# The inverse norms of queries and keys, computed one behind the other on VectorE, in a kernel of linear attention and six local attention layers

## What is computed

```
def attn_layer(x, Wqkv, qs, ksc, Wo):
    q, k, v = split(x @ Wqkv)                 # 16 heads of 64 each
    q = q / max(norm(q), 1e-12) * qs          # per token and head
    k = k / max(norm(k), 1e-12) * ksc
    q = q * cos * scale + rotate_half(q) * sin * scale
    k = k * cos / scale + rotate_half(k) * sin / scale
    out = local_attention(q, k, v)            # windows of 32, own and the one before
    return out @ Wo
```

## Time and profile before

| | |
|---|---|
| time, median of 3 runs | 2012.22 us (2008.62 to 2013.55) |
| the profiled execution | 2012.52 us, its span 2010.7 us |
| mean granted clock of TensorE, share of full speed | 0.969 |
| busy: TensorE, VectorE, ScalarE, GpSimd | 90%, 77%, 58%, 72% |
| instructions in the trace | 85596 |

### The profile page before, as it was taken

One profiled execution on the slowest core, in us unless ns is written; L12 is line 12 of the kernel. 1 busy time (PEld: TensorE's weight loads), 2 busy tenths in 40 slices (PEclk: granted clock), 3 DMA queues, 4 the chain that ended last, 5 costly groups with the idle time before them and its releaser, 6 DMA issues. The chain is left out here.

```text
span 2010.7 us, 85596 instructions
## 1 busy us (share of the span) xinstructions
PE 1805.9 (90%) x34280; PEld 1311.9 (65%) x34280; DVE 1557.0 (77%) x2776; ACT 1164.3 (58%) x1966; POOL 1455.2 (72%) x967
## 2 busy tenths in 40 slices
PE   7774689999999999999999999999999999999995
PEld 3453466676776666766666666667676667676764
DVE  4764688887888878888788788887887888878864
ACT  2311356666666666666666666666666666666662
POOL 3221688877887778777877787778777877787771
PEclk9875899999999999999999999999999999999997
DMA  4000122223222223222223322233222232222220
GB/s 151 2 3 1 44 65 65 59 54 86 73 70 53 55 63 91 59 70 63 61 53 84 77 68 55 52 82 81 63 58 59 63 86 63 70 63 55 55 58 22
DMA packets 93581, 123.43 MB, mean 61 GB/s; under 512 B 27760, under 2 KB 41808, under 8 KB 93392
## 3 DMA queue, kind: packets, MB, share of 16 engines
q1 hardware_dynamic: 93232, 122.42, 24.2%
q10 hardware_dynamic: 288, 0.13, 0.0%
HBM read 20.74 MB, written 1.05 MB: 11 GB/s over the span
## 5 line engine op out<-in xcount | busy, mean ns | idle before, releaser
L999 POOL TENSOR_TENSOR across<-unit,turns 128x1024 f32<-128x1024 f32 x192 | 497.4, 2591 | 279.7 <-issue 268.4
L1006 POOL TENSOR_TENSOR rotated<-along,across 128x1024 f32<-128x1024 f32 x192 | 496.7, 2587 | 14.2
L1151 DVE TENSOR_REDUCE sums<-squares 128x16 f32<-128x1024 f32 x192 | 234.2, 1220 | 173.2 <-ACT squares L1054 173.1
L1247 PE MATMUL turn<-identity,rotated 128*128 128x128 f32 x1536 | 205.2, 277 | 36.4 <-POOL rotated L1006 36.4
L1247 PEld LDWEIGHTS turn<-identity,rotated 128*128 128x128 f32 x1536 | 172.6, 141 | 98.9 <-issue 83.4
L1032 POOL TENSOR_TENSOR along<-unit,turns 128x1024 f32<-128x1024 f32 x96 | 228.3, 2378 | 0.0
L1352 PE MATMUL proj_a<-w_qkv,shift_a 128*128 128x512 f32 x384 | 189.9, 617 | 36.4 <-DVE unit L1176 30.1
L1113 ACT COPY val<-proj_a 128x1024 f32<-128x1024 f32 x96 | 97.2, 1013 | 181.3 <-PE proj_a L1352 181.3
L1377 PEld LDWEIGHTS att<-o_t,w_o 128*128 128x128 f32 x1536 | 188.0, 193 | 6.1 <-issue 1.0
L1377 PE MATMUL att<-o_t,w_o 128*128 128x128 f32 x1536 | 188.3, 276 | 0.0
L1280 PE MATMUL proj_a<-w_qkv,shift_a 128*128 128x512 f32 x384 | 183.5, 601 | 4.3 <-POOL shift_a L988 3.0
(11 more groups left out here) (203 smaller groups left out, 3445.2 us busy)
## 6 DMA issues: line engine op xcount, KB each, us to landing
v_win<-val SPq DMA_DIRECT2D x1536, 64.0 KB, 2.0
w_qkv<-wqkv_dram SPq DMA_DIRECT2D x18, 512.0 KB, 3.8
w_o<-wo_dram SPq DMA_DIRECT2D x6, 512.0 KB, 4.6
where<-positions_dram SPq DMA_DIRECT2D x1, 2048.0 KB, 11.4
w_ffn<-ffn_dram SPq DMA_DIRECT2D x12, 170.5 KB, 2.3
w_ffn<-ffn_dram SPq DMA_DIRECT2D x6, 192.0 KB, 2.3
x_tok<-x_dram SPq DMA_DIRECT2D x4, 256.0 KB, 4.3
out_dram<-final SPq DMA_DIRECT2D x4, 256.0 KB, 2.4
```

Of the source, the lines that this page charges most:

```text
L999: pool.tensor_tensor(a[:, :, ::-1, :], u, table, ALU.mult).then_inc(acrossed[j], 1)
L1006: pool.tensor_tensor(rotated[j][:, :, :], along[j][:, :, :], across[j][:, :, :], ALU.add).then_inc(rotated_in[j], 1)
L1151: dve.tensor_reduce(sums[:, j, :], squares[j][:, :, :], AX.X, ALU.add).then_inc(summed[j], 1)
L1247: mm = pe.transpose(bank[:, TILE * (i % 4):TILE * (i % 4) + TILE], buffer[:, TILE * i:TILE * i + TILE], identity[:, :])
```

## The change

VectorE's part is reordered. The inverse root is computed twice, on 16 heads each, with the nine operations for the queries right behind the queries' sum of squares, and the nine for the keys behind the keys' sum. The order of VectorE in a step becomes: sum (queries), root (queries), `divide_out` twice, `unite` (queries), sum (keys), root (keys), `unite` (keys), and then as before. The semaphore `rooted` becomes one for each. All other engines' lists are unchanged.

```
-        rooted = sem("rooted")
+        rooted = [sem("q_rooted"), sem("k_rooted")]
...
                     def sum_squares(j):
                         dve.wait_ge(squared[j], p + 1)
-                        after(dve, rooted, ROOT_OPS * p)
+                        after(dve, rooted[j], ROOT_OPS * p)
...
+                    def root(j):
+                        dve.wait_ge(summed[j], p + 1)
+                        after(dve, united[j], p)
+                        inverse_root(dve, range(ROOT_OPS), sums[:, j, :], sums_min[:, j, :], inv_norm[:, j, :],
+                                     [w[:, j, :] for w in root_work], magic[:, j, :], rooted[j], ROOT_OPS * p)
+
                     def unite(j):
-                        dve.wait_ge(rooted, ROOT_OPS * p + ROOT_OPS)
+                        dve.wait_ge(rooted[j], ROOT_OPS * p + ROOT_OPS)
...
                     if live["p"]:
                         sum_squares(0)
-                        sum_squares(1)
+                        root(0)
                     if live["b"]:
                         divide_out(0)
                         divide_out(1)
                     if live["p"]:
-                        dve.wait_ge(summed[0], p + 1)
-                        dve.wait_ge(summed[1], p + 1)
-                        after(dve, united[1], p)
-                        inverse_root(dve, range(ROOT_OPS), sums[:, :, :], sums_min[:, :, :], inv_norm[:, :, :],
-                                     [w[:, :, :] for w in root_work], magic[:, :, :], rooted, ROOT_OPS * p)
                         unite(0)
+                        sum_squares(1)
+                        root(1)
                         unite(1)
```

## The result

| | before | changed |
|---|---|---|
| time, median | 2012.9 us (4 runs, 2008.6 to 2014.4) | 2782.5 us (4 runs, 2781.8 to 2783.8) |
| ratio to before | 1 | 1.383, 95% interval 1.381 to 1.385 |
| span of the profiled execution | 2010.7 us | 2780.1 us |
| mean granted clock | 0.969 | 0.861 |

The change makes the kernel slower by 770 us, 8.0 us in each of the 96 steps; 2744 us was forecast. First the changed kernel's page, busy time by engine (it answers to the earlier trace rows), and the groups by line that changed most (they answer to the earlier trace rows). In the changed file lines behind the edit are shifted: L1250 is the former L1247, L1355 the values' projection, L1362 the narrowing, L1374 the spread of the rstd, L1237 the keys' `along`.

A forecast was written before the change was run, and what follows sets the result against it. TensorE, busy 90% of the span, was taken to set the path, with the keys' `unit` deciding. 2012.5 us plus 590 for the late `unit` plus 141 for the clock gave 2744 us; range 2575 to 2900.

The forecast's parts named there:

- The likeliest case: VectorE's keys' root is blocked once by each GpSimd queries' product, then runs free; 83% chance, 2744 us.
- three products: GpSimd's `across`, `along` and `rotated` of the queries, run without a break, 7.10 us in the step before the change.
- the walk: The forecast's step-by-step timing of VectorE, GpSimd and TensorE through one changed step, ending with TensorE going on at S + 15.56.
- S: The moment in a step when VectorE starts the queries' sum of squares; other times, in us, are counted from it.
- one-meeting rival: After one blocked operation VectorE runs the keys' whole root through while GpSimd waits; 2176 us, 6% chance.
- no-meeting rival: The keys' root on VectorE is not blocked by GpSimd at all; 0.4 us a step, 2051 us, 6% chance.
- The term for the late `unit`: TensorE, behind the values' projection, waits for the keys' `unit`: 6.15 us a step with copies, 590 us over 96 steps.
- 0.15 for copies: Average us a step for queries' root operations on VectorE stretched beside GpSimd's short copies.
- The term for the clock: After idling 5.8 us TensorE works at a lower clock: 1.47 us a step, 141 us; bounds 0 and 2.5 us a step.
- What was called hidden: Later centred scores (VectorE) and ScalarE work taken at 0, at most 32 us; `along` gain and GpSimd idle off the path.
- The opposite rival: Faster: TensorE's waits for the queries' `unit` and `rotated` go, 66 us, giving 1946 us; 3% chance.
- The point of decision: S + 9.56, TensorE's instruction behind the values' projection: if the keys are united before it, nothing is lost there.

The follow-up runs named there:

- e3: Changed kernel with the keys' root rewritten as ten operations, each reading at most one tensor from SBUF, the other from PSUM: 2142.6 us, 1.066 of the kernel before.
- e4b: Changed kernel with 12 matmuls that nobody reads on TensorE behind the values' projection, filling its idle gap: 2566.7 us, 1.278 of the kernel before.
- e1: Changed kernel with GpSimd holding back the queries' `across` until the keys' root is done: 2276.2 us, 1.132 of the kernel before.
- e2: Kernel before with two separate roots, both ahead of both `unite`: 2304.5 us, 1.146 of the kernel before.

## Why the prediction was right

**The meeting.** The likeliest case said that a root operation meets each of the three products once, and that the root is free behind them. So it is, and in all 96 steps: L90 and L94 take 1.24 and 1.19 us in the mean of 192, with the queries' instances near 0.2 us, which leaves 2.2 to 2.3 us for the mean of the keys', and their maxima are 2.28 and 2.20; L96 and L98 never take over 0.18 us. The times of the walk hold too: queries united at S + 5.55 (5.63 forecast), `across` at S + 5.68 (5.76), `rotated` over at S + 12.80 (12.98). It also left open whether L92 or L94 meets the third product; it is L94, so five operations are left behind the products instead of six. The one-meeting rival (2176 us) and the no-meeting rival (2051 us) both fall with L90 and L94 at 2.2 us; e3, whose root meets nothing, came out at 2143, above the latter, as it has an operation more, waits for a bank, and waits 42 us for `hidden` behind the keys' `along`.

**The term for the late `unit`.** TensorE goes on at S + 15.28 in the odd step and S + 15.42 in the even one (1549.11 - 1533.69), where S + 15.56 and 0.15 for copies were forecast. Put at 590 us, measured 556 by e4b, 0.36 us a step too large. The keys are united at S + 15.13 in both steps, 0.33 us before the walk's S + 15.46, since the products ended 0.18 us earlier and one operation less stood behind them; the 0.15 us for copies did not come, and TensorE went on 0.15 and 0.30 us behind the keys' `unit`, where 0.10 was taken. The operations themselves, 0.175 us with seams of 0.035, were sized well.

**The term for the clock** was the mis-sized one: 141 us forecast, 216 measured. The step that failed is taking the loss of one group (1.47 us) as the loss of a step. The lower clock outlasts the first group: in the odd step the narrowing loses 1.44 us, the centring 0.5 and Wo 1.3, in the even one the spread 0.6 and Wo 1.1. Its stated upper bound of 2.5 us a step held it (2.25). The two errors went opposite ways, -34 and +75 us; with the 2 us by which e4b's kernel before was below the 2012.5 us of the sum, that is the 38 us between 2744 and 2782. So the mechanism was right, and part of the nearness of the number is luck.

**What was called hidden.** The centred scores and ScalarE's part were taken at 0; ahead of L1386 (1528.93, the end of Wo at 1529.10) TensorE waits for nothing, and over all steps it waits 7.8 us for ScalarE's `probs` instead of 3.7, so they nearly are. The 0.98 us of the keys' `along` did go (1.22 us in the mean, 1.73 before) and bought nothing, as forecast. GpSimd's idle time ahead of `across` went from 2.9 to 7.1 us a step (686.1 us by 96, queries and keys together). It was forecast to move from the queries' `across` to the keys'; instead it grew ahead of the queries' (5.78 us in the odd step, 3.98 in the even one, 2.80 before) and came anew ahead of the keys' (2.41 us), as each step is 8 us longer with the same work. Two steps from S to S took 52.57 us, 26.3 each, a little over the 24.5 to 26 forecast.

**The opposite rival.** The point of decision, the keys united before S + 9.56, was missed by 5.6 us. Its price was also too high: of the 66 us, only the 0.35 to 0.38 us a step by which the values' projection starts earlier (35 us) were seen to come out, since the wait for `heads_out` took the place of that for `rotated`. e3, whose root meets nothing, misses it too (keys united at S + 10.16), so neither form of the second root that was tried gets there.

**Where my understanding was short** is in the expectations of e1 and e2: I had looked for meetings at the place the edit touched and not at the other side of the step, where the queries' root now met the tail of GpSimd's list.
